# Joining 32-row blocks of a triangular inverse with 32x32 products on TensorE instead of masked 128-row products

## The chip, the cores and the metric

The kernel runs on one core of one Trainium2 chip. The metric is the device time of one launch in microseconds (us); before the change it is 2464.01 us, the median of three runs (2460.34 to 2464.86).

## The reference

Input is 8 sequences of 512 tokens of width 256. The first layer is a gated delta-rule attention with 8 heads of width 128, followed by a small MLP; the second is a mixture of 8 experts with top-2 routing after a 20-round Sinkhorn normalisation. What matters here is the recurrence of the first layer, for each head:

```
def step(Sst, inp):
    q_t, k_t, v_t, a_t, b_t = inp
    Sst = Sst * a_t[..., None, None]
    kv = jnp.einsum('bhd,bhde->bhe', k_t, Sst)
    delta = (v_t - kv) * b_t[..., None]
    Sst = Sst + jnp.einsum('bhd,bhe->bhde', k_t, delta)
    o_t = jnp.einsum('bhd,bhde->bhe', q_t, Sst) * scale
    return (Sst, o_t)
```

The kernel does not run it token by token. It takes 128 tokens at a time; within such a tile the deltas of all tokens solve a triangular system per head, so the kernel needs X, the inverse of a unit lower triangular 128x128 matrix for each of 8 heads, and multiplies with it. What TensorE takes as its left operand is a transposed matrix, so Y, the transpose of X, is what the multiplication by the inverse reads.

## The kernel before

The launch has three phases. Up to about 143 us weights are split and the normalised input is transposed. From there to about 1610 us the attention runs over 32 tiles of 128 tokens, called steps t = 0 to 31. The rest is the routing and the experts, which the change doesn't touch.

A step is software-pipelined: while tile t goes through the state update, tile f = t + 1 goes through its front (projections, norms, products of keys and queries, the start of its inverse), and tile t - 1 goes through its tail (output projection, MLP). Each engine runs its instructions in the order in which its `step` function in the code lists them, and semaphores tie the engines together. There is no planner; an instruction that waits holds everything behind it on its engine. The name of a semaphore tells its event: `x4_loaded`, `t_ready`, `y_ready` and so on.

The inverse of a tile is made in four stages.

1. 16x16 diagonal blocks. The 64 blocks (8 per head, 8 heads) are brought by DMA into one block per partition (`lanes`, VectorE) and inverted there. Results go back by DMA to the diagonal of x4 (X, SyncE's queue) and of y4 (Y, ScalarE's queue, `blocks_y`).
2. 16-row pairs. VectorE makes the off-diagonal 16x16 block of each 32-row block (`pair_products`, `pair_inverse`), DMAs put it into x4 and y4. After this both hold complete inverses of the four 32x32 diagonal blocks. The DMAs are in `lanes_to_blocks` and `pairs_to_blocks` (lines 1081 to 1119).
3. Level 5 joins blocks of 32 rows to blocks of 64. TensorE multiplies over all 128 rows for each head: `level_t` (line 2021, product at L2035, 64 columns) into PSUM `ps_inva`; VectorE multiplies by a mask that keeps the blocks wanted and writes `ti` (L1750); `level_x` (L2052) into `ps_invb`; VectorE adds x4 and writes xi (L1758); ScalarE has copied the other half of x4 to xi (`copy_x`, L1419); then `level_y` (L2063) transposes the whole of xi against the identity, and ScalarE copies the result to yi (`copy_y`, L1424).
4. Level 6 joins the two blocks of 64: `level_t` again with 64x64 operands (L2037), ScalarE copies to ti (`copy_last_t`, L1431), `level_x` (L2054), and ScalarE completes yi (`copy_last_y`, L1436). The state update (`state_u`, L2069) then reads yi.

A float32 product is issued to TensorE as two weight loads and two matmuls, a transpose as one of each; so 8 heads give 16 pairs of weight load and matmul in L2035, L2052, L2037 and L2054, and 8 pairs in L2063. Other lines of TensorE in a step: L788 are projections (6 matmuls each), L2015 products of keys and queries, L2103 and L2113 the transposes of the output and its projection (`tail_o`, `tail_wo`), L2120 the transpose ahead of the MLP (`tail_m`), L2130 and L2140 the MLP. On VectorE L1813 (`tail_o`) makes what L2103 transposes; L1830 (`tail_m`) makes what L2120 transposes, from a root that GpSimd computes once VectorE has the output projection (L1822, L1824); L1731 starts `pair_products`, whose data come by the DMAs of L1087 and L1088.

Of the kernel before, what the change touches and what calls it, by code (L numbers as in the profile page):

```python
# [29 lines left out]
P = 128  # L30
# [12 lines left out]
L0, LEVELS = 5, 7  # L43
# [62 lines left out]
def left(a, l, halves=2):  # L106

    w = 1 << l
    return a.rearrange("p (b s) -> p b s", s=halves * w)[:, :, 0:w]


# [5 lines left out]
def program(nc, x, Wq, Wk, Wv, Wb, Wa, A_log, dt_bias, Wg, o_norm_w, Wo, W_fc, W_proj,  # L117
# [13 lines left out]
    with ExitStack() as ctx:  # L131
# [11 lines left out]
        level_mask = sb("level_mask", [P, 1, P // 2])  # L143
# [84 lines left out]
        iota_i = u_s[:, 0:2 * P].rearrange("p (n t) -> p n t", n=2).bitcast(I32)  # L228
        xor, lower = u_s[:, 2 * P:3 * P], u_s[:, 3 * P:4 * P]
# [32 lines left out]
        xy_stored, x4_loaded, y4_loaded, xcopied = (sem(n) for n in ("xy_stored", "x4_loaded", "y4_loaded", "xcopied"))  # L262
# [11 lines left out]
        x_ready = [sem(f"x_ready{g}") for g in range(G)]  # L274
# [39 lines left out]
        N_NORM, N_ROW, N_O, N_LANE, N_PAIR, N_BLOCKS, N_LATE, N_CONST = 13, 8, 15, 13, 4, NB16 + NB32, 34, 4  # L314
# [692 lines left out]
        def _(sp):  # L1007
# [49 lines left out]
            def blocks_to_lanes(f, q, more):  # L1057
# [15 lines left out]
                if not (isinstance(f, int) and f == 0):  # L1073
                    for g in range(G):
                        sp.wait_ge(inv_filled[0][g], 2 * f)
                        sp.sem_inc(sp_turn, 1)
# [4 lines left out]
            def lanes_to_blocks(f):  # L1081
# [7 lines left out]
                if not (isinstance(f, int) and f == 0):  # L1089
                    for g in range(G):  # L1090
                        sp.wait_ge(x_ready[g], f)
                        sp.sem_inc(sp_turn, 1)
                    sp.wait_ge(xcopied, f)
                    sp.sem_inc(sp_turn, 1)
                for b in range(NB16):
# [4 lines left out]
            def pairs_to_blocks(f):  # L1100
# [9 lines left out]
                for m in range(NB32):  # L1110
# [4 lines left out]
                sp.sem_inc(sp_turn, 1)  # L1115
                for m in range(NB32):
# [53 lines left out]
            sp.wait_ge(consts, 16)  # L1170
# [14 lines left out]
        def _(pool):  # L1185
            pool.memset(ones[:, :], 1.0).then_inc(consts, 1)
            pool.memset(state[:, :], 0.0).then_inc(consts, 1)
            pool.iota(iota_i[:, 0, :], pattern=[[0, P]], base=0, channel_multiplier=1).then_inc(consts, 1)
            pool.iota(iota_i[:, 1, :], pattern=[[1, P]], base=0, channel_multiplier=0).then_inc(consts, 1)
# [3 lines left out]
            pool.wait_ge(consts, 7)  # L1193
# [4 lines left out]
            pool.affine_select(out=lower, in_=ones[:, :], compare_op=ALU.is_gt, fill=0.0, base=0,  # L1198
                               pattern=[[-1, P]], channel_multiplier=1).then_inc(consts, 1)
            pool.affine_select(out=ident[:, :], in_=ones[:, :], compare_op=ALU.is_equal, fill=0.0, base=0,  # L1200
                               pattern=[[1, P]], channel_multiplier=-1).then_inc(consts, 1)
            pool.wait_ge(consts, 11)
            pool.tensor_copy(eye4[:, :].rearrange("p (h n) -> p h n", h=HG), over_heads(ident[:, :])).then_inc(consts, 1)
            pool.memset(lane_x[:, :, :], 0.0).then_inc(consts, 1)
            pool.wait_ge(consts, 13)
# [139 lines left out]
        def _(act):  # L1345
# [54 lines left out]
            right = lambda a, l: a.rearrange("p (b s) -> p b s", s=2 << l)[:, :, 1 << l:2 << l]  # L1400

            def blocks_y(f):
                act.wait_ge(xy_stored, 16 * f + 16)
                act.wait_ge(consts, 16)
                if not (isinstance(f, int) and f == 0):
                    for g in range(G):
                        act.wait_ge(x_ready[g], f)
# [5 lines left out]
            def copy_x(t, first):  # L1413
                if not first:
                    for g in range(G):
                        act.wait_ge(inv_filled[1][g], 3 * t)
                act.wait_ge(x4_loaded, 16 * N_BLOCKS * (t + 1))
                act.wait_ge(y21_stored, 16 * 4 * (t + 1))
                A(right(xi[:, :], L0), right(x4[:, :], L0), ACT.Copy).then_inc(xcopied, 1)  # L1419

            def copy_y(t, l):
                for g in range(G):
                    act.wait_ge(inv_filled[1][g], 3 * t + 2 * (l - L0) + 2)
                    A(yi[:, g * GW:(g + 1) * GW], psI[1][g][:, :], ACT.Copy).then_inc(y_ready[g], 1)  # L1424
# [530 lines left out]
        def _(pe):  # L1955
# [65 lines left out]
            def level_t(t, p, l):  # L2021
# [4 lines left out]
                for g in range(G):  # L2026
                    x = x4 if l == L0 else xi
                    if l > L0:
                        pe.wait_ge(x_ready[g], t + l - L0)
# [228 lines left out]
```

## Time and profile before

| | |
|---|---|
| median of 3 runs | 2464.01 us |
| profiled execution: span | 2462.6 us |
| attention phase in it | 143.35 to 1610 us |
| TensorE matmul busy | 2298.8 us, 93% |
| VectorE busy | 1812.0 us, 74% |
| ScalarE busy | 1155.7 us, 47% |
| GpSimd busy | 758.1 us, 31% |
| DMA, mean | 95 GB/s |

The profiled execution is told by its span, from the first to the last instruction; no other time of that execution was recorded. The median of the runs lies 1.4 us above the span. In the profile PE is TensorE's matmul, PEld its weight load, DVE VectorE, ACT ScalarE, POOL GpSimd and SPq the DMA queue of SyncE. "x16" behind a row is the number of instructions in it.

### The profile page before, as it was taken

The numbers are of one execution on the slowest core, as the hardware profiler recorded it, in microseconds if no ns is written. First come the engines' busy times: TensorE is split into PE (matmuls) and PEld (weight loads), VectorE is DVE, ScalarE is ACT, GpSimd is POOL, SyncE is SP. The second block draws the span as 40 slices with busy tenths as digits, with TensorE's granted clock in tenths as the row PEclk, the third lists the DMA queues.
The fourth block names the chain that finished last, engine by engine and source line by source line (L and its number), as shares of the span: only waits on it lengthen the run. The fifth ranks groups of instructions, "written<-read, shape, count | busy, mean of one in ns | idle before, by whom it ended". The sixth has DMA issues, their size and how long they took to land.

```text
span 2462.6 us, 51218 instructions
## 1 busy us (share of the span) xinstructions
PE 2298.8 (93%) x15387; PEld 2069.8 (84%) x15387; DVE 1812.0 (74%) x4354; ACT 1155.7 (47%) x2416; POOL 758.1 (31%) x1562
## 2 busy tenths in 40 slices
PE   4679999999999999999999999777599999999998
PEld 4568988899889889888898898666599999999887
DVE  6577887887887878878878877377666676667553
ACT  2334454444444444544444443455555455555442
POOL 0113233332332332333323323100234434434332
PEclk9889999999999999999999999856799999999999
DMA  5321212212212112122122121589544545444340
GB/s 189 99 36 39 52 35 46 42 35 48 41 35 52 37 40 51 35 46 42 35 48 41 35 50 28 175 299 315 180 160 151 172 152 175 162 159 164 132 128 18
DMA packets 369742, 232.92 MB, mean 95 GB/s; under 512 B 261612, under 2 KB 343920, under 8 KB 360464
## 3 DMA queue, kind: packets, MB, share of 16 engines
q1 hardware_dynamic: 317136, 200.35, 28.1%
q0 software_dynamic: 11280, 29.31, 4.1%
q10 hardware_dynamic: 41264, 2.51, 1.1%
q8 instruction: 31, 0.51, 0.1%
q14 instruction: 31, 0.25, 0.0%
HBM read 176.19 MB, written 57.67 MB: 95 GB/s over the span
## 4 chain that ended last, share of the span: by engine, by line
PE 85%; DVE 6%; ACT 2%; DMA 2%; issue 2%; SPq 2%; POOL 0%; DVEq 0%; ACTq 0%; POOLq 0%
PE ps_front L788 13%; PE ps_back L2069 11%; PE ps_inva L788 9%; PE ps_invb L788 9%; PE ps_back L788 8%; PE ps_back L2130 5%; PE ps_front L2015 5%; PE ps_back L2113 5%; PE ps_back L2140 4%; PE ps_inva L2035 2%; PE ps_invb L2052 2%; PE ps_front L2008 2%; PE ps_invb L2054 1%; PE ps_inva L2037 1%; PE ps_inva L424 1%
## 5 line engine op out<-in xcount | busy, mean ns | idle before, releaser
L652 DVE TENSOR_TENSOR w_lo<-w_raw,w_hi 128x512 fp32r<-128x512 f32 x288 | 190.1, 688 | 3.9
L788 PE MATMUL ps_back<-w_hi,eh_hi 128*128 128x256 f32 x624 | 180.1, 289 | 3.2 <-DVE eh_lo L662 3.2
L788 PE MATMUL ps_back<-w_lo,eh_hi 128*128 128x256 f32 x624 | 176.5, 283 | 0.0
L788 PE MATMUL ps_back<-w_hi,eh_lo 128*128 128x256 f32 x624 | 176.5, 283 | 0.0
L740 ACT ACTIVATE w_hi<-w_raw 128x512 fp32r<-128x512 f32 x288 | 169.6, 626 | 0.0
L752 ACT ACTIVATE sact<-ps_inva 128x512 f32<-128x512 f32 (+1 forms) x96 | 49.7, 517 | 236.3 <-PE ps_inva L788 236.3
L1374 ACT ACTIVATE v_s<-ps_front 128x512 f32<-128x512 f32 x64 | 38.1, 595 | 247.3 <-PE ps_front L788 247.3
L1374 ACT ACTIVATE g_s<-ps_front 128x512 f32<-128x512 f32 x64 | 38.3, 598 | 221.0 <-PE ps_front L788 210.6
L1279 POOL TENSOR_SCALAR xrow_v<-bag 128x1 f32<-128x1 f32 x31 | 6.8, 219 | 423.8 <-DVE bag L1850 423.8
L788 PE MATMUL ps_inva<-xT_hi,w_hi 128*128 128x512 f32 (+1 forms) x384 | 135.3, 352 | 1.7 <-DVE xT_lo L657 1.7
L2015 PE MATMUL ps_front<-kqT_t 128*128 128x256 f32 x512 | 126.7, 391 | 10.5 <-ACT kqT_t L1398 7.7
L2069 PE MATMUL ps_back<-state,kqT_t 128*128 128x128 f32 x1024 | 132.7, 283 | 3.0 <-DVE r_s L1772 1.8
L788 PE MATMUL ps_inva<-xT_lo,w_hi 128*128 128x512 f32 (+1 forms) x384 | 135.0, 352 | 0.0
L788 PE MATMUL ps_inva<-xT_hi,w_lo 128*128 128x512 f32 (+1 forms) x384 | 134.7, 351 | 0.0
L788 PE MATMUL ps_invb<-xT_hi,w_lo 128*128 128x512 f32 (+1 forms) x384 | 134.3, 350 | 0.0
L788 PE MATMUL ps_invb<-xT_lo,w_hi 128*128 128x512 f32 (+1 forms) x384 | 134.2, 350 | 0.0
L788 PE MATMUL ps_invb<-xT_hi,w_hi 128*128 128x512 f32 (+1 forms) x384 | 134.2, 349 | 0.0
L1690 DVE SCALAR_TENSOR_TENSOR aP<-ps_front,nbh,dT 128x256 f32<-128x256 f32 x256 | 108.5, 476 | 34.0 <-PE ps_front L2015 34.0
L2069 PEld LDWEIGHTS ps_back<-state,kqT_t 128*128 128x128 f32 x1024 | 126.7, 195 | 8.1 <-DVE r_s L1772 2.0
L680 DVE TENSOR_TENSOR eh<-sact,ps_inva 128x512 f32<-128x512 f32 (+1 forms) x96 | 56.5, 588 | 95.2 <-ACT sact L752 95.2
L788 PE MATMUL ps_front<-wqk_hi,hT_hi 128*128 128x512 f32 x256 | 107.3, 419 | 18.7 <-ACT k_s L1374 13.2
L2130 PE MATMUL ps_back<-rows,tails 128*128 128x128 f32 x1024 | 124.2, 280 | 0.5 <-ACT rows L1441 0.5
(399 smaller groups left out, 7119.2 us busy)
## 6 DMA issues: line engine op xcount, KB each, us to landing
w_raw<-wts_d SPq DMA_DIRECT2D x72, 1024.0 KB, 5.3
wts_d<-prep SPq DMA_DIRECT2D x96, 256.0 KB, 3.9
dT<-alphaT_d SPq DMA_DIRECT2D x32, 512.0 KB, 3.6
prep<-L_ffn_W_gate_dram SPq DMA_DIRECT2D x32, 256.0 KB, 3.3
prep<-L_ffn_W_up_dram SPq DMA_DIRECT2D x32, 256.0 KB, 3.7
prep<-L_ffn_W_down_dram SPq DMA_DIRECT2D x32, 256.0 KB, 4.4
x_all<-L_attn_x_dram SPq DMA_DIRECT2D x4, 1024.0 KB, 10.0
hTr<-hT_d SPq DMA_DIRECT2D x32, 128.0 KB, 3.6
```

The costliest lines, as they stand in the source:

```text
L652: V.tensor_tensor(piece(w_lo[p], m).bitcast(F32R), piece(w_raw, m), piece(w_hi[p], m), ALU.subtract).then_inc(split[n], 1)
L680: V.tensor_tensor(eh[:, s, 0:rows], sact[:, s, 0:rows], psG[2 * s + 1][:, 0:rows], ALU.mult).then_inc(eh_ready[s], 1)
L740: A(piece(w_hi[p], m).bitcast(F32R), piece(w_raw, m), ACT.Copy).then_inc(hi_ready[n], 1)
L752: A(sact[:, s, 0:rows], psG[2 * s][:, 0:rows], ACT.Silu).then_inc(sact_ready[s], 1)
L788: ins = MM(out_, w[a].bitcast(F32R), x[b].bitcast(F32R), start=start and n == 0, stop=stop and n == 2)
L1374: A((k_s[:, q], q_s, v_s, g_s)[n // 2][:, n % 2 * GW:(n % 2 + 1) * GW], psF[u % 2][:, :], ACT.Silu).then_inc(front_evac[u % 2], 1)
L1690: ins = V.scalar_tensor_tensor(aP[:, q, c], psF[u % 2][:, h * 2 * P:(h + 1) * 2 * P].rearrange("p (a n) -> p a n", a=2), nbh[:, q, c:c + 1 ...
L2015: last = MM(ps[:, h * 2 * P:(h + 1) * 2 * P], kqT[:, c, 0, :], kqT[:, c].rearrange("p a n -> p (a n)"), start=True, stop=True)
L2069: last = MM(ps[:, h * DK:(h + 1) * DK], left(g * HG + h), right(g * HG + h), start=True, stop=True)
L2113: last = MM(ps[:, 0:D], cols(oT, h), wo[:, h, :], start=h == 0, stop=h == H - 1)
L2130: last = MM(ps[:, fb * P:(fb + 1) * P], wfc[:, k, c:c + P], mT[:, k * P:(k + 1) * P], start=k == 0, stop=k == KD - 1)
L2140: last = MM(ps[:, 0:D], h[:, b].bitcast(F32R), w.bitcast(F32R), start=fb == 0 and n == 0, stop=fb == FB - 1 and n == 2)
```

## The change

Level 5 is done block by block. In `block_t` TensorE makes, for each head and for m = 0 (rows 0 to 63) and m = 1 (rows 64 to 127), one product of 32x32 operands; VectorE copies the two results without a mask (`block_t` on VectorE, 32 partitions each). In `block_xy` three products per head follow: the new block of X for m = 0, and the new block of Y for m = 0 and m = 1, which is the product with its operands swapped, so no transpose of the whole is made. VectorE copies the X block into x4 (`block_x`), ScalarE the two Y blocks into y4 (`copy_y`). xi and yi are no longer used for the result: level 6 (`half_t`, `half_y`) and the state update read x4 and y4. `copy_x`, the mask and its making are gone. The X of the last 32 rows isn't needed in any product, so two of eight DMAs of the 16x16 blocks and one of four of the pair blocks aren't issued. Since the state update now reads y4 itself, the DMAs that write the pair blocks to y4 wait for the state update of the tile before.

```diff
-            def level_t(t, p, l): ...
-            def level_x(t, l): ...
-            def level_y(t, l):
-                if l == L0:
-                    pe.wait_ge(xcopied, t + 1)
-                for g in range(G):
-                    pe.wait_ge(x_ready[g], t + l - L0 + 1)
-                    for h in range(HG):
-                        last = nc.tensor.transpose(psI[1][g][:, h * P:(h + 1) * P], cols(xi, g * HG + h), ident[:, :])
-                    last.then_inc(inv_filled[1][g], 1)
+            def block_t(t, p):
+                pe.wait_ge(x4_loaded, 16 * N_XBLOCKS * (t + 1))
+                pe.sem_inc(pe_turn, 1)
+                for h in range(H):
+                    for m in range(2):
+                        r = 2 * W32 * m
+                        even, odd = slice(r, r + W32), slice(r + W32, r + 2 * W32)
+                        ins = MM(psI[0][m][odd, h * W32:(h + 1) * W32], aP[even, p, h, 0, odd], cols(x4, h)[even, even], start=True, stop=True)
+                        if h == H - 1:
+                            ins.then_inc(inv_filled[0][m], 1)
+
+            def block_xy(t):
+                pe.wait_ge(y4_loaded, 16 * N_BLOCKS * (t + 1))
+                for m in range(2):
+                    r = 2 * W32 * m
+                    even, odd = slice(r, r + W32), slice(r + W32, r + 2 * W32)
+                    pe.wait_ge(t_ready[m], 2 * t + 1)
+                    pe.sem_inc(pe_turn, 1)
+                    for h in range(H):
+                        c = slice(h * W32, (h + 1) * W32)
+                        y, tm = cols(y4, h)[odd, odd], ti[odd, c]
+                        if m == 0:
+                            MM(psI[1][m][odd, c], y, tm, start=True, stop=True)
+                        last = MM(psI[1][m][even, GW // 2 + h * W32:GW // 2 + (h + 1) * W32], tm, y, start=True, stop=True)
+                    last.then_inc(inv_filled[1][m], 1)
+
+            def half_t(t, p): ...        # level 6 as before, from x4, behind x_ready and t_ready[1]
+            def half_y(t): ...           # level 6 as before, from y4, behind y_ready[0] and [1] of copy_y
 ...
-                level_t(t, p, L0)
+                block_t(t, p)
 ...
-                level_x(t, L0)
+                block_xy(t)
                 if more:
                     project(f, q, 4)
-                level_y(t, L0)
-                level_t(t, p, L0 + 1)
+                half_t(t, p)
                 if more:
                     project(f, q, 5)
                 if tail:
                     tail_m(t - 1)
-                level_x(t, L0 + 1)
+                half_y(t)
 ...
+            def block_t(t):
+
+                for m in range(2):
+                    r = slice(2 * W32 * m + W32, 2 * W32 * (m + 1))
+                    dve.wait_ge(inv_filled[0][m], 2 * t + 1)
+                    V.tensor_copy(ti[r, 0:GW // 2], psI[0][m][r, 0:GW // 2]).then_inc(t_ready[m], 1)
+
+            def block_x(t):
+
+                dve.wait_ge(inv_filled[1][0], 2 * t + 1)
+                V.tensor_copy(x4[W32:2 * W32, :].rearrange("p (h n) -> p h n", h=H)[:, :, 0:W32],
+                              psI[1][0][W32:2 * W32, 0:GW // 2].rearrange("p (h n) -> p h n", h=H)).then_inc(x_ready, 1)
 ...
-                for b in range(NB16):
+                for b in range(XB16):
 ...
-                for m in range(NB32):
+                for m in range(XB32):
```

TensorE's instructions in the second half of a step, from the products of keys and queries on; ps_inva holds the first product of the join, ps_invb the second, and x4, y4 read x, y here. A row with x8 has one product per head. Before:

```order
L2015 MATMUL ps_front<-kqT_t 128x256 x4
L2023 REGISTER_ALU
L2035 MATMUL ps_inva<-x,aP 128x64 x8
L1990 REGISTER_ALU
L2103 MATMUL ps_back<-ident,o_s 128x128 x4
```

And after:

```order
L1969 MATMUL ps_front<-kqT_t 128x256 x4
L1982 MATMUL ps_inva<-x,aP 32x32 x16
L2059 MATMUL ps_back<-ident,o_s 128x128 x8
```

The place in the order is the same; 8 products of 128 rows have become 16 of 32.

The second place on TensorE is behind the output projection (ps_back<-tails,oT), up to the second 64-row product. Before:

```order
L2113 MATMUL ps_back<-tails,oT 128x256 x4
L2044 ISA
L2052 MATMUL ps_invb<-ti,y 128x64 x8
L1986 REGISTER_ALU
L788 MATMUL ps_front<-wvg_hi,hT_hi 128x512
...
L788 MATMUL ps_front<-wvg_hi,hT_lo 128x512
L2063 MATMUL ps_invb<-ident,xi 128x128 x8
L2037 MATMUL ps_inva<-xi,aP 64x64 x8
```

And after:

```order
L2069 MATMUL ps_back<-tails,oT 128x256 x8
L1997 MATMUL ps_invb<-ti,y 32x32
L1998 MATMUL ps_invb<-y,ti 32x32
...
L1998 MATMUL ps_invb<-y,ti 32x32 x9
L782 MATMUL ps_front<-wvg_hi,hT_hi 128x512
...
L782 MATMUL ps_front<-wvg_hi,hT_lo 128x512
L2008 MATMUL ps_inva<-x,aP 64x64 x8
```

Here 8 products and 8 transposes have become 24 products of 32 rows; the 64-row product follows the projection directly.

## Rows read from the trace of the kernel before

**Rows 1.** The page, busy time in us of each engine

```profile
PE 2298.8 (93%) x15387; PEld 2069.8 (84%) x15387; DVE 1812.0 (74%) x4354; ACT 1155.7 (47%) x2416; POOL 758.1 (31%) x1562
```

**Rows 2.** Stretches: window, its length, busy us of PE, PEld, DVE, ACT, POOL, then clock

```profile
1000.00:1045.20 45.20, 44.77 (x323) 40.54 (x322) 37.13 (x98) 21.17 (x46) 15.16 (x38) 1.00 0.22 43
1500.00:1545.20 45.20, 39.24 (x268) 35.82 (x267) 31.39 (x75) 14.63 (x33) 14.82 (x37) 0.89 0.23 45
```

**Rows 3.** Chain that ended last, one step: start us, us, what

```profile
412.15 1.73 PE ps_inva L2035 x16
...
457.30 1.73 PE ps_inva L2035 x16
...
465.10 1.73 PE ps_invb L2052 x16
466.83 1.45 PE ps_front L788 x6
468.27 0.87 PE ps_invb L2063 x8
469.15 1.07 PE ps_inva L2037 x16
470.22 1.59 PE ps_front L788 x6
...
483.69 1.39 PE ps_front L788 x6
```

**Rows 4.** Timeline of the step (start, us); groups of weight loads (busy, mean ns)

```profile
465.83 0.86 PEld L2052 LDWEIGHTS ps_invb<-ti,y 128*128 128x128 f32 x7
...
469.08 1.00 PEld L2037 LDWEIGHTS ps_inva<-xi,aP 64*64 64x64 f32 x16 [0.17 <-issue]
469.08 1.14 PE L2037 MATMUL ps_inva<-xi,aP 64*64 64x64 f32 x16
...
L2052 PEld LDWEIGHTS ps_invb<-ti,y 128*128 128x128 f32 x512 | 62.1, 192 | 3.3 <-issue 1.7
...
L2037 PEld LDWEIGHTS ps_inva<-xi,aP 64*64 64x64 f32 x512 | 32.1, 135 | 5.4 <-issue 5.4
```

**Rows 5.** Timeline: last gated outputs on VectorE, first transpose of them

```profile
457.32 0.86 DVE L1813 SCALAR_TENSOR_TENSOR o_s<-o_s,or,gw 128x128 f32<-128x128 f32 x3
458.87 1.05 PE L2103 MATMUL ps_back<-ident,o_s 128*128 128x128 f32 x8
```

**Rows 6.** Timeline and chain: the MLP's input, in a full step and in the last

```profile
470.32 0.35 DVE L1830 TENSOR_SCALAR rows<-rows,mrow_r 128x256 f32<-128x256 f32 x1 [0.65 <-POOL mrow_r L1262]
471.65 0.38 PE L2120 MATMUL ps_back<-ident,rows 128*128 128x128 f32 x2
...
1594.14 0.04 issue
1594.18 0.45 PE ps_back L2120 x2
```

**Rows 7.** Timeline and chain: the DMA of pair data and its first reader

```profile
480.02 0.52 SPq L1088 DMA_DIRECT2D xi<-xy_d  x1
484.95 1.22 DVE L1731 TENSOR_TENSOR yi<-xi 128x1024 f32<-128x1024 f32 x1
...
126.08 4.21 DMA xi<-xy_d
```

**Rows 8.** Timeline and chain: the last DMAs to x4, level 5 of steps 0 and 1

```profile
497.05 1.96 SPq L1112 DMA_DIRECT2D x<-x_d  x4
...
140.57 2.74 DMA x<-x_d
143.35 2.00 PE ps_inva L2035 x16
186.28 1.86 PE ps_inva L2035 x16
```

**Rows 9.** Groups of one step, VectorE: count, busy us, mean ns

```profile
L1758 DVE TENSOR_TENSOR xi<-x,ps_invb 128x256 f32<-128x256 f32 x2 | 0.7, 412 | 0.0
```

More of the change, by code:

```diff
@@ L42 @@
 GW = HG * DK
-L0, LEVELS = 5, 7
+W32 = 32
 FB = F // P
@@ L1115, in pairs_to_blocks @@
                 sp.sem_inc(sp_turn, 1)
+                if not (isinstance(f, int) and f == 0):
+                    for g in range(G):
+                        u = BU_U + g
+                        sp.wait_ge(back_filled[u % 2], b_filled(f - 1, u))
+                        sp.sem_inc(sp_turn, 1)
                 for m in range(NB32):
@@ L1398, in copy_T @@
                     A(kqT[:, n * HG:(n + 1) * HG, a, :], psF[u % 2][:, :].rearrange("p (h n) -> p h n", h=HG), ACT.Copy).then_inc(front_evac[u % 2], 1)
-            right = lambda a, l: a.rearrange("p (b s) -> p b s", s=2 << l)[:, :, 1 << l:2 << l]
             def blocks_y(f):
                 act.wait_ge(xy_stored, 16 * f + 16)
[L1404 to L1407, printed above, removed]
+                act.wait_ge(consts, N_ZEROED)
                 for b in range(NB16):
@@ L1411, in blocks_y, with copy_y @@
                                   xy_d[lanes_of(b), 1, :].rearrange("h (i n) -> i h n", i=W16)).then_inc(y4_loaded, 16)
[L1413 to L1424, printed above, removed]
+            def copy_y(t):
+                for m in range(2):
+                    r = 2 * W32 * m
+                    act.wait_ge(inv_filled[1][m], 2 * t + 1)
+                    A(y4[r:r + W32, :].rearrange("p (h n) -> p h n", h=H)[:, :, r + W32:r + 2 * W32],
+                      psI[1][m][r:r + W32, GW // 2:GW].rearrange("p (h n) -> p h n", h=H), ACT.Copy).then_inc(y_ready[m], 1)
             HP = P // 2
@@ L1493, in tail_x, with step @@
                 evac(t + 1, BU_XT, xfT[:, :])
-            def step(t, p, more, ahead, tail, first=False):
+            def step(t, p, more, ahead, tail):
                 f, q = t + 1, 1 - p
@@ L1504, in step @@
                 scaled_qs(t, p)
-                copy_x(t, first)
                 if more:
@@ L1725, in pair_products @@
                 dve.wait_ge(pair_loaded, 16 * 3 * f + 16 * 3)
-                if not (isinstance(f, int) and f == 0):
-                    for g in range(G):
-                        u = BU_U + g
-                        dve.wait_ge(back_filled[u % 2], b_filled(f - 1, u))
                 ch = Chain(dve, lane_dve, (N_LANE + N_PAIR) * f + N_LANE)
@@ L2057, in level_y @@
[L2057 to L2063 removed]
+                        last = MM(psI[1][g][0:HP, h * HP:(h + 1) * HP], ti[HP:P, c * HP:(c + 1) * HP], cols(y4, c)[HP:P, HP:P], start=True, stop=True)
```

121 lines of the change are left out of this document (34 added, 87 removed).

## The prediction

> **What bounds the kernel now.** I read the page first: TensorE is busy 93% of the span, VectorE 74% [rows 1]. In the chain L2035 comes again after 45.15 us (412.15, 457.30) [rows 3], which is the length of a step; in a stretch of 45.2 us TensorE is busy 44.8 us at a granted clock of 1.00, the 2.4 GHz level, and VectorE 37.1 [rows 2]. The chain that ended last is, through a full step, one TensorE piece behind the other, the products of the join among them [rows 3]. So a microsecond taken from TensorE in a step is a microsecond of the step, as long as nothing that TensorE waits for has less room than that. This is the question of the second half of the work: where is the room.
>
> The window at 1500 us shows TensorE busy only 39.2 of 45.2 us [rows 2]: in the last two steps the front work runs out. The first step is different as well, below.
>
> **What goes.** In the chain a step spends 1.73 us on L2035, 1.73 on L2052 and 0.87 on the transposes L2063 [rows 3]: 4.33 us. L2037 (1.07 us) and its twin L2054 stay as they are.
>
> **What comes.** 16 products in block_t and 24 in block_xy, as two pairs of weight load and matmul each: 32 + 48 = 80 pairs, 32 columns of weights and 32 columns streamed. No row of before has such a pair, so it is priced from the two widths that are there. Seven loads of 128 columns take 0.86 us from the start of the first to the end of the last; one lasts 0.192, so a pair comes every (0.86 - 0.19) / 6 = 0.112 us. Sixteen of 64 columns take 1.00 us with 0.135 for the last, so one every 0.0577 us [rows 4]. Half the columns save 0.054 us; half again, at the same slope, should save 0.027 and give 0.031 us. 80 x 0.031 = 2.47 us.
>
> The ends of this price: not below zero, and not above 0.0577, since a narrower pair has no reason to be slower than a 64-column one. Both widths fit a straight line with about 4 ns left at zero columns, which is what a cost by columns looks like and what a fixed cost per pair does not. But two points always lie on a line, and a floor anywhere under 0.0577 would be invisible in them. I take 0.031 because the slope between the rows, 0.84 ns a column, is so close to one column in 1/1.2 GHz = 0.83 ns that a floor is not yet to be seen.
>
> The Trainium skill ("TensorE: Matmul & The Clock Gate", section "Wait — 56ns, not 53.3ns?") has a rule against this change: with hardware decode off, some 62 ns go by per matmul however small it is. By it the 80 pairs would take 4.96 us and a step would grow. The trace speaks against it here, since the 64-column pairs already come every 57.7 ns [rows 4]. The same section's other floor, 25 ns from start to start, lies under the 31 ns and would change nothing.
>
> Then the change of shape. Around the 64-row products something is lost: L2037's 16 pairs would take 16 x 0.0577 = 0.92 us and stand with 1.07 in the chain, and the projection behind them takes 1.59 us where the same six matmuls take 1.39 elsewhere [rows 3]; the weight load also sat idle for 0.17 us in front [rows 4]. That is 0.15 + 0.20 = 0.35 us for going into small products and out again. Before, a step did this twice; now it does it four times: 0.70 us more. Bounds: nothing (if only the 64-row form pays it) to twice that.
>
> Sum for a full step: 2.47 + 0.70 - 4.33 = -1.16 us.
>
> **Is there room for it.** TensorE arrives earlier at four things.
> - The gated outputs. VectorE's last L1813 ends at 458.18, the first transpose L2103 starts at 458.87: 0.69 us [rows 5]. When a wait does bind, TensorE starts 0.04 us behind VectorE, as in the last step [rows 6], so the room is 0.65. block_t arrives 1.73 - 32 x 0.031 - 0.35 = 0.39 us earlier. It fits, 0.26 left.
> - The MLP's input. VectorE's L1830 ends at 470.67 and waits for GpSimd's root, which starts when the output projection is done; TensorE's L2120 starts at 471.65 [rows 6]. Room 0.98 - 0.04 = 0.94 us. The root's start moves with block_t by 0.39, TensorE by 1.16, so 0.77 of it are used. It fits with 0.17 us to spare, the tightest of all. If it didn't, half_y, the MLP's products and the state update would queue behind it.
> - The pair data. Their last DMA is issued at 480.02 and VectorE reads at 484.95. In the pipeline's filling, where it binds, the data took 4.21 us to come [rows 7], so they are there at about 484.23: room 0.72, used 0.77 (the lanes in front move with block_t, VectorE's reader with everything). It may cost VectorE 0.05 us, which isn't on the chain.
> - x4 for the next block_t. The work between the state update and it isn't touched. The last of four DMAs is issued at 497.05 + 3/4 x 1.96 = 498.52 and takes 2.74 us [rows 8], so 501.26, against 457.30 + 45.15 = 502.45 where it is read. One of the four is gone, which adds 0.49 us of room. The new wait of the y4 DMAs for the state update costs nothing: the state update was over 15 us earlier; queued behind it on SyncE's queue are only those DMAs and the store of xf.
>
> On VectorE the two masked products become two copies and the two additions one copy of the same 256 columns, one operation of 412 ns less [rows 9]; the copy of X must be there before half_t, where it used to be before the transposes. block_x is queued behind the sum of squares as L1758 was, and project(4), 1.45 us [rows 3], lies between block_xy and half_t. So nothing is late there: TensorE's block_xy takes 48 x 0.031 + 0.35 = 1.83 us instead of 1.73, and the copy has the projection to hide under. ScalarE loses copy_x and copies half the columns in copy_y; all of that lies beside TensorE's work, and I count it as nothing. So do the two DMAs less to x4 and the consts that are no longer made, under the loading of the weights.
>
> **The total.** Steps 1 to 29 are full: 29 x 1.16 = 33.6 us. In step 0 TensorE waits for the inverse of the next tile: from its L2035 at 143.35 to that of step 1 at 186.28 [rows 8] are 42.9 us with TensorE partly idle, so only the DMA less counts, 0.5 us. In the last two steps I count half, 1.2 us. Together -35.3 us, on a span of 2462.6: 2427.3, and 1.4 more for what lies between span and median: **2428.7 us**.
>
> **The rivals.**
> A. A small product costs what a larger one costs: TensorE pays a fixed price per pair. For it: nothing in the trace is faster than 57.7 ns, and the change makes 80 pairs of 40. Against it: the halving from 112 to 58. At 57.7 ns the pairs take 4.62 us, the step grows by 4.62 + 0.70 - 4.33 = 0.99 us, and the kernel by 29 x 0.99 + 1 = 30: 2494 us. It is slower from (4.33 - 0.70) / 80 = 45 ns a pair on.
> B. The products overlap. In block_t the products of m = 0 and m = 1 use different rows and different output rows, and they alternate. For it: the matmul and the load of the next weights already start together, both at 469.08 [rows 4]. If pairs cost next to nothing, the room above ends the gain: 0.65 us at the gated outputs and 0.94 at the MLP's input, 1.59 a step, 29 x 1.59 + 1.7 = 48: 2416 us. The Trainium skill (the same page, "What overlaps and what doesn't") says that weight loads overlap running matmuls where their row groups differ; that is this rival's mechanism, and no row of before shows it.
> C. Something beside TensorE holds the step. If the root on GpSimd or the pair data take what is gained behind block_t, only block_t's 0.39 us stay: 29 x 0.39 + 1 = 12: 2452 us. Against it the four rooms above; for it that two are nearly used up.
> D. Going into 32-row products costs more than into 64-row ones, 0.70 us a time instead of 0.35: the step gains 0.46 us, 2450 us; with a pair at 37 ns as well it gains nothing.
>
> **How the numbers follow.** Forecast 0.55 (2422 to 2437 by itself), A 0.13, B 0.15, C 0.08, D 0.09. A measurement of this kernel tells 0.2% from no change, 5 us. Faster are the forecast, B, C and about half of D: 0.82; D's other half is within 5 us: 0.05; A is slower: 0.13. The range leaves out A and the worst of D: 2414 to 2454 us.
>
> **What will show it.** In the chain of a full step block_t at about 1.3 us, block_xy at 1.8, the transposes gone, a step of 44.0 us. Weight loads of 32 columns every 31 ns; at 45 or more A is right, at 25 or less B. The projections behind block_xy and half_t at 1.59 us, else the price of the change of shape is wrong. An idle time of TensorE before L2120's successor, put down to VectorE's row, would show that the MLP's input had no room. If the granted clock in a full step falls from 1.00, none of the prices hold.

## The result, and the profile after

The changed kernel took 2507.41 us (median of 4 runs, 2502.64 to 2509.18), the kernel before 2464.44 us beside it (2460.34 to 2466.17): 1.0178 times as long, 95% interval [1.0164, 1.0191]. I had forecast 2428.7 us, with 2454 as the upper end. The kernel became 43 us slower instead of 35 us faster.

The page after: busy time of the engines, the two queues that fetch instructions (packets, MB, share), the chain by engine, and TensorE's group with the most idle time.

```profile
PE 2271.4 (91%) x16667; PEld 2002.6 (80%) x16667; DVE 1816.3 (72%) x4317; ACT 1126.1 (45%) x2384; POOL 760.1 (30%) x1559
q14 instruction: 95, 0.78, 0.1%
q8 instruction: 32, 0.52, 0.1%
PE 49%; DVE 25%; issue 11%; POOL 6%; DMA 3%; ACT 3%; SPq 1%; POOLq 1%; DVEq 1%; ACTq 0%
L2025 PE MATMUL ps_back<-state,kqT_t 128*128 128x128 f32 x1024 | 152.9, 311 | 58.2 <-DVE r_s L1726 57.0
```

TensorE is busy 27 us less than before [rows 1], so the products did get cheaper. But it idles 57.0 us for r_s on VectorE, which is not the work that was changed. Another row is new: queue 14 carried 95 instruction packets; before it was this:

```profile
q14 instruction: 31, 0.25, 0.0%
```

64 packets more, for a loop of 14 rounds that goes back to its start 13 times. Where they fall is in the steps: one after the other they last 43.5 and about 50.5 us (from TensorE's first product of delta_products to the next step's), where before each took 45.15 [rows 3]. VectorE's loop holds two steps a round. The timeline of after around the branch at 453.4 us (start, us, engine, line; in brackets the idle time before and what ended it):

```profile
453.36 1.22 DVE L1759 TENSOR_REDUCE os<-r_s 128x8 f32<-128x1024 f32 x1
456.30 1.22 DVE L1614 TENSOR_REDUCE ssk<-u_s 128x8 f32<-128x1024 f32 x1 [1.73 <-issue]
460.19 2.16 DVE L1726 SCALAR_TENSOR_TENSOR r_s<-ps_back,sc,v_s 128x128 f32<-128x128 f32 x8 [2.67 <-issue]
461.37 2.50 PE L2025 MATMUL ps_back<-state,kqT_t 128*128 128x128 f32 x10 [4.36 <-DVE r_s L1726]
```

VectorE stands still for 1.73 and 2.67 us although all its inputs are there ("issue": it waits for nothing the profile shows), and TensorE waits 4.36 us behind it. On queue 14 packets of 8192 bytes start at 454.4, 458.2 and 460.6, and two more in the same round at 494.6 and 529.6: VectorE fetches its own program again, each of the 13 times that it goes back.

In the built programs the branch into the loop is VectorE's instruction 326 before and 318 after, and the loop is 325 and 317 instructions long. The change took eight instructions from VectorE ahead of the loop, and eight from a step pair in it. The Trainium skill ("Runtime: NRT & Kernel Launch", section "Instruction fetch mechanics") gives 256 instructions to 16 KiB, so a packet of 8192 bytes is 128 instructions; that is the unit in which the experiments below move the loop. The trace agrees: the last three packets of this round start when VectorE is 9, 134 and 264 instructions past the branch.

The granted clock fell with it, as two neighbouring windows of 45.2 us show (length, busy us of PE, PEld, DVE, ACT, POOL, clock, then DMA): 0.92 in the window in which TensorE waited, 1.00 in the other.

```profile
1000.00:1045.20 45.20, 40.44 (x317) 34.92 (x316) 32.80 (x85) 16.93 (x37) 15.23 (x38) 0.92 0.16 27
1045.20:1090.40 45.20, 44.01 (x375) 38.48 (x374) 38.27 (x100) 21.05 (x46) 15.22 (x38) 1.00 0.23 50
```

### The profile page after: what moved, and what is told of

It reads as the page before. It is cut to its first block, busy times and chain, and to the rows that moved or that the text cites. A ratio compares the mean times of both kernels' runs of the same rounds, so it can differ in the third digit from the quotient of the medians.

```text
span 2507.2 us, 53383 instructions
## 1 busy us (share of the span) xinstructions
PE 2271.4 (91%) x16667; PEld 2002.6 (80%) x16667; DVE 1816.3 (72%) x4317; ACT 1126.1 (45%) x2384; POOL 760.1 (30%) x1559
## 4 chain that ended last, share of the span: by engine, by line
PE 49%; DVE 25%; issue 11%; POOL 6%; DMA 3%; ACT 3%; SPq 1%; POOLq 1%; DVEq 1%; ACTq 0%
PE ps_inva L782 9%; PE ps_invb L782 9%; PE ps_back L782 8%; PE ps_back L2069 5%; PE ps_back L2086 4%; PE ps_front L1969 3%; PE ps_back L2025 3%; DVE state L1746 3%; DVE dT L1637 2%; DVE rows L1809 2%; DVE xi L1698 2%; DVE xi L1692 2%; DVE yi L1691 2%; DVE o_s L1767 1%; DVE yi L1697 1%
## 5 line engine op out<-in xcount | busy, mean ns | idle before, releaser
L2025 PE MATMUL ps_back<-state,kqT_t 128*128 128x128 f32 x1024 | 152.9, 311 | 58.2 <-DVE r_s L1726 57.0
L2025 PEld LDWEIGHTS ps_back<-state,kqT_t 128*128 128x128 f32 x1024 | 145.5, 222 | 65.4 <-DVE r_s L1726 60.3
L1387 ACT ACTIVATE kqT_t<-ps_front 128x512 f32<-128x512 f32 x128 | 70.5, 595 | 191.3 <-PE ps_front L1962 191.3
L2086 PE MATMUL ps_back<-rows,tails 128*128 128x128 f32 x1024 | 124.5, 281 | 0.5 <-ACT rows L1419 0.5
```

The lines of the kernel that those rows point to most:

```text
L1387: A(kqT[:, n * HG:(n + 1) * HG, a, :], psF[u % 2][:, :].rearrange("p (h n) -> p h n", h=HG), ACT.Copy).then_inc(front_evac[u % 2], 1)
L2025: last = MM(ps[:, h * DK:(h + 1) * DK], left(g * HG + h), right(g * HG + h), start=True, stop=True)
L2086: last = MM(ps[:, fb * P:(fb + 1) * P], wfc[:, k, c:c + P], mT[:, k * P:(k + 1) * P], start=k == 0, stop=k == KD - 1)
```

## The experiments

**The loop's place.** Each of the first four adds instructions ahead of an engine's loop that only count up a semaphore:

```diff
         def _(dve):
             V = nc.vector
+            for _ in range(8):
+                dve.sem_inc(dve_turn, 1)
```

Eight on VectorE of the changed kernel:

> The changed kernel with 8 instructions more on VectorE (increments of a semaphore nobody waits for) at the very start of its program, long before its loop; nothing else differs. Theory 1: VectorE's loop starts in the last few instructions of an 8 KB piece of its instruction stream and so touches four pieces, too many to be kept, and each round of the loop (two steps) fetches them again; 8 instructions more put the loop's start behind the boundary. Then the fetches on queue 14 in the loop (5 a round) go, every step takes 43.5 us like the undisturbed ones of the changed kernel, and the time is 2507 - 14 x 7 = about 2410 us. Theory 2: the long step comes from the work itself (small products, the colder clock of TensorE, waits at the join); 8 idle instructions change nothing: 2507 us, steps still 43.5 and 50.6.

2429.59 us (2426.93 to 2434.18), ratio to the kernel before 0.9865 [0.9849, 0.9881]. Queue 14 is back at 30 packets, none of them in the loop, and every step lasts 44.0 us. Eight instructions that do nothing made the kernel 78 us faster, which is 6.0 us for each return to the loop's start. I had expected 2410 us, from steps of 43.5; those stand only between long ones.

```profile
q14 instruction: 30, 0.25, 0.0%
```

120 on VectorE of the kernel before:

> The kernel before with 120 instructions more on VectorE at the start of its program. 120 is 128 - 8: it moves the loop's start, modulo a piece of 128 instructions, to where it was 8 instructions earlier, as the change has it. Theory 1: the kernel before gets the same disease, some 5 instruction fetches a round on queue 14, a stall at each of 14 loop ends, and about 60 to 100 us more: 2525 to 2565 us. Theory 2: 120 increments at the start, while VectorE waits for its input anyway, cost nothing: 2464 us.

2548.44 us, ratio 1.0354 [1.0336, 1.0371]; 96 packets, steps of 45.4 and 51 us. The stall has nothing to do with the change itself: the kernel before catches it as well.

Eight on ScalarE (pe_turn instead) of the changed kernel:

> The changed kernel with the 8 extra instructions on ScalarE instead of VectorE. Theory 1: VectorE's stream is where it was, 2507 us and steps of 43.5 and 50.6 us. A rival to it, that any small shift in the start of the program or ScalarE's own stream cures the stall: about 2410 us.

2504.48 us in one run, 95 packets. It is VectorE's loop.

80 and 60 on VectorE of the changed kernel:

> The changed kernel with 80 instructions more on VectorE. Its loop has 317 instructions, 2.48 pieces of 128; it fits in three pieces only if it starts within the first 67 of a piece. By theory 1 the start without padding is 1 to 8 instructions ahead of a boundary, with 80 more it is 72 to 79 behind one, so the loop touches four pieces again: the stalls are back, around 2507 us, though they fall elsewhere in the loop. If only the loop's first instructions near a boundary matter and not the number of pieces, the stall is gone: 2410 us.

> The changed kernel with 60 counts ahead of VectorE's loop. Theory of the pieces: the loop of 317 instructions then begins 52 to 59 instructions behind a boundary of 128, ends at 369 to 376 and so still lies in three pieces: no fetch in the loop, a step of 44.0, 2430 us. With 80 counts it lay in four, and the fetches were there. Rival, the fetches hang on something other than the pieces (the number of instructions ahead): fetches in each round, 2445 or more.

With 60: 2433.62 us in one run, 31 packets, steps of 44.0. With 80: the fetches are there (96 packets), but 2449.39 us in one run, not 2507: steps of 43.5 and 46 us. So the rule on where the loop lies held in every run, and the price did not: 1.5 us a round here (89.5 against 88.0), about 6 in the result and in the kernel before with 120. VectorE's timeline with 80 shows one wait where the result has two:

```profile
444.04 1.22 DVE L1616 TENSOR_REDUCE ssk<-u_s 128x8 f32<-128x1024 f32 x1 [1.90 <-issue]
445.18 2.15 DVE L1728 SCALAR_TENSOR_TENSOR r_s<-ps_back,sc,v_s 128x128 f32<-128x128 f32 x8
```

The first wait follows the branch. The second, 2.67 us in the result and again with 120 in the kernel before, comes behind the loop's second instruction there. With 80 the third packet starts only when VectorE is 51 instructions past the branch (9 in the result), and nothing waits there. That fits a boundary between pieces two instructions behind the loop's start in the first two placements and 50 in this one (2 + 128 - 80): where it is two, VectorE has hardly any work left before it needs the next piece. This is read from three traces; no placement between them was run. A loop of 317 fits in three pieces of 128 if it begins at most 67 instructions behind a boundary. Where the boundaries lie is inferred from which runs fetched, to within eight instructions: with 8 it begins 0 to 7 behind, with 60 52 to 59, with 80 72 to 79; without, 120 to 127 behind, so it touches a fourth.

The same section of the Trainium skill ("Runtime: NRT & Kernel Launch", "Instruction fetch mechanics") says that a taken branch whose target is outside a window of two pages forces a fetch. The runs agree that a branch can. By the page's sizes that window would hold 512 instructions, four pieces of 128; here a loop in three pieces was kept and one that touched four was fetched again.

**What a 32x32 product costs.** In the changed kernel neighbouring products of block_t (m = 0 and 1) use different rows. e5 puts those of one tile together, on top of the eight counts:

```diff
-                for h in range(H):
-                    for m in range(2):
+                for m in range(2):
+                    for h in range(H):
...
+                    for h in range(H):     # block_xy: all y, tm first
                         last = MM(psI[1][m][even, ...], tm, y, ...)
```

> The changed kernel with 8 counts ahead of VectorE's loop, and the same products in another order: block_t does all of m = 0 and then all of m = 1, block_xy all products x4's block first and then all of T's. Theory: two products that differ in rows or output columns overlap (two pairs in 32 ns), two of one tile don't (one in 31.5). Then block_t takes 32 x 0.0315 = 1.0 us and 0.35 for the shape instead of 0.6 in all, block_xy 24... 48 x 0.0315 + 0.35 = 1.1 to 1.6 instead of 0.9 (its second order has 8 + 16 pairs, 24 x 2 loads and matmuls). TensorE's work grows by 0.8 to 1.4 us a step; it waits 1.2 us a step now, so the step grows by 0.2 to 0.9: 2435 to 2456 us. Rival, a price by the pair whatever the order: nothing moves, 2430.

2439.27 us, 0.9897 [0.9879, 0.9916], a step of 44.3. Timelines of block_t, first with the eight counts alone, then with one tile at a time:

```profile
845.95 0.69 PE L1984 MATMUL ps_inva<-x,aP 32*32 32x32 f32 x32
```

```profile
804.73 1.09 PE L1984 MATMUL ps_inva<-x,aP 32*32 32x32 f32 x32
```

Each group's time holds the 0.19 us of its last product. (0.69 - 0.19) / 31 = 16 ns a pair when tiles alternate, (1.09 - 0.19) / 31 = 29 ns when they don't. The second holds the change from m = 0 to m = 1, where pairs overlap; inside one tile the single matmuls of the trace start 31 to 32 ns apart. So the price I took, 31 ns, is right for one tile, and rival B's overlap is right for the order that the change has. In block_xy (m = 0) the two products of a head share their rows and differ in output columns, and they overlapped too (two pairs in about 32 ns). The Trainium skill ("TensorE: Matmul & The Clock Gate", "What overlaps and what doesn't") says that a weight load overlaps running matmuls only where row groups differ; here the trace does not agree, it shows overlap for differing columns as well.

**Where TensorE's time counts.** The step with the eight counts is 44.0 us, just what I forecast, but for another reason. Some pieces of its chain of waits, which now leaves TensorE for the rest of the step (start, us, what):

```profile
800.86 1.14 DVE o_s L1769 x5
...
802.91 1.09 PE ps_back L2061 x8
...
805.72 3.47 PE ps_back L2071 x16
809.22 0.43 DVE rows L1778
...
813.13 0.35 POOL mrow_r L1248
...
819.84 0.69 DVE lane_x L1685
...
824.10 4.38 DMA xi<-xy_d
...
833.26 1.23 DVE rows L1811
...
837.37 1.14 DVE os L1761
...
845.02 1.09 DVE o_s L1769 x4
```

TensorE is busy 85.56 of 88.00 us. Three runs ask whether its time counts at all. First the same 0.93 us taken from project(7), at the end of the step, in the changed kernel (with the eight counts) and in the kernel before (4 matmuls of 0.232 us); two thirds of that projection are left out:

```diff
-                    last = exact(MM, ps[:, :], ...)
+                    if n < 7:
+                        last = exact(MM, ps[:, :], ...)
+                    else:
+                        last = MM(ps[:, :], hT_hi..., w[0]..., ...)
```

> The changed kernel with 8 counts ahead of VectorE's loop, and 4 of the 6 matmuls of project(7) left out (the products with the lower halves, so G's second half is rounded): 0.93 us less on TensorE in a step, 4 x 0.232. Theory: a chain beside TensorE holds the step at 44.0, so most of it is lost: a step of 43.7 to 44.0, 2421 to 2430 us. Rival, TensorE holds it: 43.1, 2403 us.

> The kernel before with the same 4 matmuls of project(7) left out. Theory: before, TensorE holds the step, so it gets 0.9 us shorter, less where the rooms are used up: 44.2 to 44.4, 2436 to 2441 us. Rival, the room on other engines was used up in the kernel before too: 2455 or more.

2429.58 us, 0.9867 [0.985, 0.9883]: nothing. And in the kernel before 2470.66 us, 1.0025 [1.0006, 1.0045], a step of 45.16: nothing either, the total even 8 us longer. My theory of the kernel before fell here. TensorE simply waits 1.00 us for a row of VectorE:

```profile
851.20 0.43 PE L2150 MATMUL ps_back<-ident,rows 128*128 128x128 f32 x2 [1.00 <-DVE rows L1855]
```

The kernel before has the same wait already, only too short for the timeline to print (there the transposes are L2147):

```profile
489.62 1.32 DVE L1855 TENSOR_SCALAR rows<-rows,bag,xrow_r 128x256 f32<-128x256 f32 x1
491.06 0.43 PE L2147 MATMUL ps_back<-ident,rows 128*128 128x128 f32 x2
```

TensorE starts 0.12 us behind VectorE's row, and its records show it idle for 0.07 to 0.12 us in front of L2147 in each full step. So VectorE already held this place, though the chain named TensorE alone.

Then the same 0.93 us from project(5), between the output projection and the MLP, in the kernel before (the edit against the run just shown):

```diff
-                    if n < 7:
+                    if n != 5:
```

> The kernel before with 4 of the 6 matmuls of project(5) left out (instead of project(7)'s): the same 0.93 us of TensorE, but between the output projection and the MLP. Theory: this stretch is in the ring and had 0.94 us of room at the MLP's input, so the step gets 0.7 to 0.93 us shorter, 44.2 to 44.45: 2435 to 2442 us. Rival, VectorE or GpSimd hold the whole ring and no microsecond of TensorE counts: 2455 or more.

2437.69 us, 0.9913 [0.9897, 0.993], a step of 44.4. The same TensorE time, earlier in the step, is worth 0.75 us a step and not nothing.

The reason stands in VectorE's timeline of the kernel before. From 479.22 until the gated outputs it shows no idle time but 0.15 us, and 0.40 in front of them:

```profile
455.95 2.23 DVE L1813 SCALAR_TENSOR_TENSOR o_s<-o_s,or,gw 128x128 f32<-128x128 f32 x8 [0.35 <-POOL or L1248]
479.22 0.69 DVE L1837 TENSOR_TENSOR hid_lo<-o_s,hid_hi 128x512 fp32r<-128x512 f32 x1 [1.46 <-ACT hid_hi L1486]
483.55 0.18 DVE L1850 BATCH_NORM_AGGREGATE bag<-bst 128x2 f32<-128x6 f32 x1 [0.15 <-DVE bst L1848]
501.15 1.96 DVE L1813 SCALAR_TENSOR_TENSOR o_s<-o_s,or,gw 128x128 f32<-128x128 f32 x7 [0.40 <-POOL or L1248]
```

and with the eight counts:

```profile
800.55 2.23 DVE L1769 SCALAR_TENSOR_TENSOR o_s<-o_s,or,gw 128x128 f32<-128x128 f32 x8 [0.35 <-POOL or L1237]
822.44 0.69 DVE L1793 TENSOR_TENSOR hid_lo<-o_s,hid_hi 128x512 fp32r<-128x512 f32 x1 [0.91 <-ACT hid_hi L1464]
844.72 2.22 DVE L1769 SCALAR_TENSOR_TENSOR o_s<-o_s,or,gw 128x128 f32<-128x128 f32 x8 [0.41 <-POOL or L1237]
```

I read the step as a ring of two halves. From the MLP's hidden rows to the gated outputs VectorE has 21.9 us of work with hardly a gap (501.15 - 479.22; 22.3 with the eight counts). From there to the next hidden rows TensorE sets the pace, 23.3 us before (479.22 - 455.95) and 21.9 after (822.44 - 800.55). What is taken from TensorE outside its half bought nothing, what is taken inside did.

Where its half got shorter can be read too. From VectorE's first gated output to TensorE's first transpose of them it is 2.9 us before (455.95 to 458.87 [rows 5]) and 2.4 with the eight counts (800.55 to 802.91); over 21 steps of each trace the medians are 2.87 and 2.36. Before, TensorE came to these transposes straight from L2035; now it is through block_t early and waits 0.43 us for VectorE. So about 0.5 us of block_t's saving counts and the rest is that wait. From the end of the output projection to the MLP's input it is 6.55 before and 5.63 after, medians again: 0.9 us from block_xy and the transposes. VectorE's half grew by 0.2 to 0.4 us.

The two halves of the change, each issued twice (to the same places) with the eight counts:

```diff
-                for h in range(H):
-                    for m in range(2):
+                for h, m in [(h, m) for h in range(H) for m in range(2)] * 2:
```

```diff
-                    for h in range(H):      # block_xy
+                    for h in [*range(H)] * 2:
```

> The changed kernel with 8 counts ahead of VectorE's loop; block_t's 16 products are issued twice, to the same places: 0.5 us more on TensorE. Theory: behind block_t TensorE waits 0.43 us for the gated outputs, so it lies outside the ring: 0 to 0.1 us a step, 2429 to 2433. Rival, TensorE's time counts everywhere: 0.5 a step, 2444.

> The changed kernel with 8 counts ahead of VectorE's loop; block_xy's 24 products are issued twice, to the same places: 0.75 us more on TensorE. Theory: block_xy lies inside the ring, beside GpSimd's root for the MLP's input, behind which TensorE waits 0.27 us: the step grows by 0.75 - 0.27 = 0.5 us, 2444. Rival, the root holds this stretch with more room: under 2435.

block_t twice: 2427.72 us, 0.9862 [0.9846, 0.9878], a step of 44.0, though its group grew from 0.69 to 1.20 us. The added 0.51 us fill the wait of 0.43 at the gated outputs: a block_t up to 0.5 us slower would have cost nothing. It does not say that the 1.73 us of before would have. block_xy twice: 44.4 us in most steps, 0.4 more, which is the forecast. Its total, 2478.52 us (2452.04 to 2481.39), is not: in the profiled execution five steps last 48 to 51 us, with TensorE idle as VectorE was in the result, and this time queue 8 fetches:

```profile
817.33 0.58 PE L782 MATMUL ps_front<-wqk_hi,hT_hi 128*128 128x512 f32 x1 [2.74 <-issue]
```

```profile
q8 instruction: 80, 1.31, 0.2%
```

That is TensorE's own program: its loop is 1109 instructions long here, against 1013 in the changed kernel and 1077 with block_t twice, where the queue carried 34 packets. Why some rounds stall and others don't I have not tested.

**Trying to shorten the rest.** Four reorderings, each on top of the eight counts (e8 on the kernel before).

```diff
+                if more:
+                    lanes(f, True)      # copy, first doubling
                 if tail:
                     tail_m(t - 1)
                 if more:
-                    lanes(f)
+                    lanes(f, False)
...
+                half_y(t)               # TensorE
                 if tail:
                     tail_m(t - 1)
-                half_y(t)
```

> The changed kernel with 8 counts ahead of VectorE's loop; the copy and the first doubling of the lanes' inverse stand ahead of the MLP's input on VectorE, and half_y ahead of the MLP's input on TensorE. Theory: without the instruction fetches the step of 44.0 us is held by a chain beside TensorE, over GpSimd's root, VectorE's MLP input and the lanes queued behind it, the lanes' DMAs, the pair products, the state, and TensorE's idle time is 1.2 us a step. The lanes then end about 1 us earlier, and half_y covers the MLP input's 0.45 us more: a step of 43.0 to 43.6, 2400 to 2418 us. Rival, TensorE's own work holds the step: 2430.

> The kernel before with the reorder of lanes_early alone (its level_x of level 6 ahead of the MLP's input in place of half_y). Theory: before, TensorE holds the step, so nothing moves: 2462 us, within 4. Rival, the reorder is worth something by itself: 2440 or less.

2438.71 us, 0.989 [0.9872, 0.9909], and before 2485.97 us, 1.0086 [1.0069, 1.0103]: 9 and 23 us slower than without the reordering (2429.59 and 2463.14). half_y had been the work under which ScalarE copies the transposed MLP input; ahead of it, it left that copy bare:

```profile
L2096 PE MATMUL ps_back<-rows,tails 128*128 128x128 f32 x1024 | 124.2, 280 | 17.3 <-ACT rows L1419 17.3
```

The group had 0.5 us of idle time in the result's profile (L2086). With TensorE's order as it was and only three of VectorE's operations moved:

```diff
                     ch.link(V.tensor_reduce(t21..., prod, X, ALU.add))
+                    if w == 2:
+                        yield
...
+                rest = lanes(f) if more else ()
+                if more:
+                    next(rest)
                 if tail:
                     tail_m(t - 1)
-                if more:
-                    lanes(f)
+                list(rest)
```

> The changed kernel with 8 counts ahead of VectorE's loop; only the lanes' copy, their first product and its sum (0.6 us) stand ahead of the MLP's input on VectorE, in the 1.2 us in which it waits for GpSimd's root; TensorE's order is as it was, so half_y still covers ScalarE's copy of the transposed MLP input, which lanes_early uncovered (17.3 us of waits). Theory: the chain over the lanes holds the step, so it gets 0.3 to 0.6 us shorter: a step of 43.4 to 43.7, 2410 to 2420 us. Rival 1: the lanes aren't what holds it (the root, or the state and the gated outputs do): 2430. Rival 2: the lanes' data come too late for the gap and push the MLP's input back: 2430 to 2440.

2435.65 us, 0.9891 [0.9874, 0.9907], a step of 44.0 to 44.1, where a hold by the lanes would have given 43.4 to 43.7. The lanes are not what holds the step.

tail_xf behind the first product of pair_inverse, with a yield in the same way:

```diff
+                rest = pair_inverse(f) if more else ()
+                if more:
+                    next(rest)
                 if tail:
                     tail_xf(t - 1)
-                if more:
-                    pair_inverse(f)
+                list(rest)
```

> The changed kernel with 8 counts ahead of VectorE's loop; on VectorE tail_xf stands behind the first product of pair_inverse instead of ahead of it. There it would no longer run beside GpSimd's product over v_s (1.90 us), beside which its 128x256 operation takes 1.31 us instead of some 0.36. Theory: the step is a ring of VectorE's unbroken stretch (the MLP's hidden rows to the gated outputs, 24.5 us) and TensorE's (19.5 us); the ring gets 0.95 us shorter, until TensorE's own work stops it at about 42.8 to 43.2: a step of 43.0 to 43.5, 2400 to 2416 us. Rival 1, the operation is as long elsewhere: 2430. Rival 2, the transposes of xf come later and TensorE waits for them: 2425 to 2435.

2463.20 us, 1.0004 [0.9994, 1.0014], a step of 45.2. The wait beside GpSimd did not go, it moved to the next operation, and two longer waits came behind it (timelines of VectorE, GpSimd and TensorE):

```profile
804.09 2.24 DVE L1699 TENSOR_TENSOR yi<-xi 128x1024 f32<-128x1024 f32 x1
806.37 0.41 DVE L1812 TENSOR_SCALAR rows<-rows,bag,xrow_r 128x256 f32<-128x256 f32 x1
...
809.24 0.17 DVE L1818 TENSOR_SCALAR la<-ps_back 128x8 f32 x1 [1.08 <-PE ps_back L2115]
...
803.35 1.90 POOL L1295 TENSOR_TENSOR v_s<-v_s,sqk 128x1024 f32<-128x1024 f32 x1
...
806.91 0.44 PE L2108 MATMUL ps_back<-ident,rows 128*128 128x128 f32 x2 [1.50 <-DVE rows L1812]
```

L1699 took 1.21 us elsewhere; here it ends 1.1 us after GpSimd's product. TensorE now waits 1.50 us for the rows of xf (0.32 with the eight counts alone, at 834.62), and VectorE then 1.08 us for the logits, which TensorE makes later.

```diff
+                square_sums(t, p)
                 if more:
                     pair_inverse(f)
                 if tail:
                     tail_logits(t - 1)
-                square_sums(t, p)
+                moments(t, p)      # its copy of two scalars alone
```

> The changed kernel with 8 counts ahead of VectorE's loop; on VectorE the sum of the outputs' squares (1.22 us) stands ahead of pair_inverse instead of behind it and the logits, so GpSimd's root (6.2 us) starts about 3 us earlier and is done before VectorE asks for it. Theory of the ring: VectorE's wait of 0.41 us ahead of the gated outputs goes, and nothing else: a step of 43.6 us, 2418 us (2412 to 2424). Rival 1, TensorE or the lanes hold the step: 2430. Rival 2, the pair data come 1.2 us later and block_t waits for x4: 2440 to 2460.

2429.83 us, 0.9859 [0.9843, 0.9876], a step of 44.0. VectorE's wait at the gated outputs is gone, as forecast, and the 0.4 us are lost at once. TensorE has new waits on the way there, 0.20 us for the logits in each step and this one for x4, behind a later pair_inverse, in every second:

```profile
847.81 0.69 PE L1986 MATMUL ps_inva<-x,aP 32*32 32x32 f32 x32 [0.16 <-DMA x<-x_d]
```

It now comes to the gated outputs 2.48 us behind VectorE's first one instead of 2.36, without waiting for them: its own work is the longer path there again. How the 0.4 us divide among these was not tested. Both this run and the one before were forecast from the ring, at 43.6 and 43.0 to 43.5 us, and both missed. The ring tells which of TensorE's microseconds count; it is not shown to be the only path of 44 us, and the chain above goes by GpSimd's root and the lanes' DMAs, of which only the lanes were tried, in e9.

So no version beat the changed kernel with eight counts by more than a measurement tells: 2429.6 us, 1.35% faster than the kernel before.

## Why the prediction was wrong

- **The step that failed: the total.** It adds up what the operations on TensorE cost and counts everything on VectorE, fewer instructions included, as nothing. I never asked where an engine's program lies. The missing term is a refetch of VectorE's loop, +78 us (2507.4 against 2429.6 with eight counts). It was in no rival. Two things to ask from were at hand: a packet count of 31 on queue 14, too low for a loop that is fetched again, and the instructions that the diff takes out ahead of VectorE's loop. Without this term my forecast, 2428.7, misses by 1 us.
- **That agreement is partly luck.** "A microsecond taken from TensorE in a step is a microsecond of the step" is false: 0.93 us at project(7) are worth 0, at project(5) 0.75. I took the chain of waits, all TensorE [rows 3], for the only one; VectorE had a second path of the same length beside it, and the share of 37.1 us in 45.2 [rows 2] hid that its idle time lies almost all in the other half. TensorE's busy time fell by 1.8 us a step instead of 1.16 (2298.8 to 2241.7 us over 31 steps), and it waits some 0.8 us more; the two errors nearly cancel.
- **Price of the pairs.** 31 ns holds inside one tile (31 to 32 measured). The change's own order overlaps: 16 ns, with starts of neighbouring tiles 6 to 7 ns apart, which is also under the floor of 25 ns that the prediction set beside its 31. block_t took 0.62 us in the chain instead of my 1.34, block_xy 1.0 (809.18 to 810.21) instead of 1.83. Rival B had the overlap right, but its end of the gain, 1.59 us a step, was too far: it ended at 1.15.
- **The change of shape** is paid where I looked for it: the projections behind block_xy and half_t take 1.59 and 1.60 us from the end of the small products to their own (810.21 to 811.80, 812.94 to 814.54).
- **Rooms.** The one that I called the tightest, the MLP's input, was used up: TensorE now waits there 0.27 us of each step, behind GpSimd's root. It waits 0.43 us at the gated outputs too, where I had seen 0.26 to spare, since block_t came 1.1 us earlier and not 0.39. The 0.39 us of gain that I had counted to block_t were about 0.5; block_xy and the transposes gave the larger part. Rival C's mechanism, something beside TensorE, is true of half of the step, at a smaller price than it asked.
- **The rest.** The pair data, which I had let go as off the chain, stand in the chain with the eight counts (824.10, 4.38 us). The copies of the join and the new wait of the y4 loads stand in none that I read. Rivals A and D did not happen: neither a floor of 57.7 ns a pair nor a dearer change of shape.

## What to carry to other kernels

Before counting what an edit saves, count the instructions that it adds or removes ahead of and inside each engine's loop, and look at the rows of the instruction queues: here eight decided between +43 and -35 us. A chain of waits that is all one engine shows one of several longest paths; look for a second engine with hardly a gap over part of the step, and for places where the first one starts about 0.1 us behind it, which the views don't print as a wait. Count only what is taken from the stretch that the first one holds alone. Instructions that do nothing test the first point cheaply, and matmuls left out or issued twice the second.

## What the runs showed of the hardware

- VectorE went 14 rounds through a loop of 317 or 325 instructions without a fetch when, by the placing inferred above, it lay in three pieces of 128, and fetched 5 packets of 8192 bytes at each of 13 returns when it touched a fourth. The price was about 6 us a return in two placements, with two waits of VectorE, and 1.5 in a third, with one.
- TensorE's program comes over queue 8. With its loop at 1109 instructions (block_xy twice) there were fetches, and some steps were up to 7 us longer; at 1077 there were none. Whether length or place decides was not tested.
- Pairs of 32x32 in float32: 31 to 32 ns one after the other in one tile, 16 ns when two tiles alternate, by rows or by output columns.
- VectorE's 128x1024 product of two tiles from memory took 2.24 us beside a product of GpSimd that ran for 1.90 us, and 1.21 us alone; its 128x256 product by scalars took 1.31 us there and 0.41 elsewhere. Its products of the state with PSUM took 0.34 us each beside GpSimd's product and without it.
